# Two message-passing layers on a graph: edge pairs staged over three steps instead of five, self connection of layer 1 at later lags

## The reference

```python
def layer0(x, a, src, dst, edge_attr, edge_scalars, W):
    h = linear(x, lin1) * a                      # per node
    w = silu(edge_scalars @ fc_w1) @ fc_w2       # 224 weights per edge
    e0, e1 = edge_attr[:, :1], edge_attr[:, 1:4]
    # per edge, from h[src], w, e0 and e1: 96 scalars and 128 vectors
    mid = products(h[src], w, e0, e1)            # a cross product among them
    agg = segment_sum(mid, dst, n) / 4
    pre = self_connection(x) + linear(agg, lin2) * a
    return silu / sigmoid gates applied to pre
# layer 1: the same shape without the cross product, a mean over the edges of a node
# and a factor alpha per node in place of the gates
x = layernorm(x + layer0(...))
x = layernorm(x + layer1(x, ...))
```

## Time and profile before

| | us |
|---|---|
| median of 3 runs | 2077.51 |
| lowest and highest | 2066.84, 2082.15 |
| the profiled execution | 2061.54 (span of its trace 2059.5) |
| edges, layer 0 | 0 to about 757 |
| nodes, layer 0 | about 757 to 1097 |
| edges, layer 1 | about 1097 to 1786 |
| nodes, layer 1 | about 1786 to 2059 |

### The profile page before, as it was taken

How to read it: one execution, slowest core, us unless ns; L and a number is a source line. 1 busy time by engine, 2 the same in 40 slices (tenths; PEclk the granted TensorE clock), 3 DMA queues, 4 the chain that set the end, 5 groups by cost and what they waited for, 6 DMA issues and landing times.

```text
span 2059.5 us, 47563 instructions
## 1 busy us (share of the span) xinstructions
PE 1431.6 (70%) x10424; PEld 1270.4 (62%) x10424; DVE 1443.3 (70%) x5661; ACT 1067.1 (52%) x3600; POOL 1498.0 (73%) x2021
## 2 busy tenths in 40 slices
PE   5077887878888848778775999999999999200000
PEld 4067777767777737666654988888888888200000
DVE  5066776767777619999993766666666666199997
ACT  3033444434444317999983555555555555147676
POOL 3077877778788648888884577777777777468876
PEclk9589999999999979999997999999999999655555
DMA  9966666666666759999964677777777777499997
GB/s 388 430 150 138 135 131 136 137 137 135 131 137 138 169 128 320 322 320 319 317 237 133 165 166 174 172 170 173 175 167 171 171 172 159 80 364 406 400 390 280
DMA packets 253878, 439.88 MB, mean 214 GB/s; under 512 B 33424, under 2 KB 131152, under 8 KB 250576
## 3 DMA queue, kind: packets, MB, share of 16 engines
q1 hardware_dynamic: 150288, 306.88, 44.3%
q0 software_dynamic: 75264, 67.79, 23.8%
q10 hardware_dynamic: 28224, 64.24, 8.1%
HBM read 235.50 MB, written 203.27 MB: 213 GB/s over the span
## 4 chain that ended last, share of the span: by engine, by line
POOL 38%; issue 21%; PE 14%; ACT 9%; DMA 8%; SPq 4%; DVE 3%; ACTq 2%; POOLq 1%; another core or an unknown queue 0%; DVEq 0%
POOL table L482 16%; POOL xg L465 8%; ACT y L827 6%; DMA table<-sums,row_all 5%; POOL half_rstd L516 5%; SPq L370 3%; PE ps L642 2%; POOL gate L547 2%; PE ps L623 2%; POOL gate L538 2%; DMA dst_row<-in_dst_row 2%; ACTq L838 2%; PE ps L609 1%; PE ps L628 1%; PE ps L625 1%
## 5 line engine op out<-in xcount | busy, mean ns | idle before, releaser
L482 POOL DMA_INDIRECT table<-sums,row_all x392 | 627.9, 1602 | 306.9 <-issue 131.2
L764 ACT COPY msg<-ps 128x192 f32<-128x192 f32 (+1 forms) x196 | 57.4, 293 | 691.9 <-PE ps L642 555.9
L827 ACT ACTIVATE y<-res,norm 128x160 f32<-128x160 f32 x756 | 331.9, 508 | 133.3 <-ACT y L827 62.1
L975 DVE SCALAR_TENSOR_TENSOR x1g<-ps,a_all,x1g 128x160 f32<-128x160 f32 x392 | 132.3, 379 | 200.2 <-PE ps L662 130.3
L465 POOL DMA_INDIRECT xg<-in_x_rows,src_all x196 | 201.0, 1025 | 59.6 <-issue 57.2
L465 POOL DMA_INDIRECT xg<-x_rows,src_all x196 | 195.3, 997 | 65.0 <-issue 59.4
L623 PE MATMUL ps<-weights,midT 128*128 128x128 f32 (+1 forms) x784 | 161.7, 290 | 95.6 <-DVE msg L935 93.9
L1055 DVE BATCH_NORM_STATS2 stats<-res 128x6 f32<-128x160 f32 x784 | 195.6, 310 | 2.6
L930 DVE TENSOR_TENSOR pe<-ps,ea_all 128x192 f32<-128x192 f32 x196 | 69.4, 354 | 170.4 <-ACT msg L764 73.6
L623 PEld LDWEIGHTS ps<-weights,midT 128*128 128x128 f32 x784 | 124.5, 200 | 103.1 <-issue 95.6
L516 POOL TENSOR_TENSOR half_rstd<-var,minus_half 128x8 f32<-128x8 f32 x98 | 165.5, 1688 | 14.2
(11 more groups left out here) (115 smaller groups left out, 4465.1 us busy)
## 6 DMA issues: line engine op xcount, KB each, us to landing
...
```

The source lines that it names most:

```text
L482: pool.indirect_dma_start(out=table[l], out_offset=bass.IndirectOffsetOnAxis(ap=row_all[:, at:at + 1], axis=0), in_=sums[j % 4][:, t, 0:W] ...
L827: last = nc.scalar.activation(y[u][:, t, :], res[u][:, t, :], ACT.Identity, scale=rstd[u][:, t:t + 1], bias=shift[u][:, t:t + 1])
L975: last = stt(x1g[v][:, 2 * b + t, :], n1_ps[:, t, :], a, x1g[v][:, 2 * b + t, :], ALU.mult, ALU.add)
```

## The change

The lists of `run_stages` in the edge stages get other lags and another order. A pair's `turn_mid` and `copy_midT` go from lag 2 to lag 1, at the end of the lists; `second_map` and `copy_message` from lag 3 to 2, at their head; `message_vectors` and `message_sum` from 4 to 2, behind `compare`; `sum_pair` and `copy_sums` from 5 to 3. In layer 1 the self connection goes from lags 0, 1 and 2 to 3, 4, 5 and 6 and the store of the base from 4 to 10; x1g is used as a ring of eight buffers in place of four, with a semaphore for each.

```diff
--- before.py
+++ after.py
@@ -286,8 +286,8 @@
         s_z1 = sem("self_connection_added")
         s_x1z = sem("z_of_x1_together")
         s_n1 = sem("self_connection_done_layer1")
-        s_x1 = sem4("x1_loaded")
-        s_bstore = sem4("base_stored")
+        s_x1 = [sem(f"x1_loaded{u}") for u in range(RING)]
+        s_bstore = [sem(f"base_stored{u}") for u in range(RING)]
         s_base = [sem(f"base_loaded{u}") for u in range(RING)]
         s_nT = sem("nodes_turned")
         s_nTsb = sem("nodes_turned_copied")
@@ -377,20 +377,18 @@
                     sp.dma_start(table[1][bass.ds(m * GROUP, GROUP), :].rearrange("(p t) c -> p (t c)", t=T),
                                  zeros[:, 0:T * LAYERS[1]["ROW"]]).then_inc(s_zero[1], 16)
 
+                def store_base(g, m, u):
+                    sp.wait_ge(s_z1, 2 * (g + 1 - NG))
+                    sp.sem_inc(s_sptick, 1)
+                    sp.dma_start(base_rows[bass.ds(m * GROUP, GROUP), :].rearrange("(p t) c -> p (t c)", t=T),
+                                 x1g[u][:, :, :].rearrange("p t c -> p (t c)")).then_inc(s_bstore[u], 16)
+
                 def load_x1(g, m, u):
 
-                    v = u % 4
-                    wait_count(sp, s_bstore[v], landed(g - 4, first_of(v, 4), 4))
+                    wait_count(sp, s_bstore[u], landed(g - RING, first_of(u, RING), RING))
                     sp.sem_inc(s_sptick, 1)
-                    sp.dma_start(x1g[v][:, :, :].rearrange("p t c -> p (t c)"),
-                                 x1_rows[bass.ds(m * GROUP, GROUP), :].rearrange("(p t) c -> p (t c)", t=T)).then_inc(s_x1[v], 32)
-
-                def store_base(g, m, u):
-
-                    v = u % 4
-                    sp.wait_ge(s_z1, 2 * (g + 1 - NG))
-                    sp.dma_start(base_rows[bass.ds(m * GROUP, GROUP), :].rearrange("(p t) c -> p (t c)", t=T),
-                                 x1g[v][:, :, :].rearrange("p t c -> p (t c)")).then_inc(s_bstore[v], 16)
+                    sp.dma_start(x1g[u][:, :, :].rearrange("p t c -> p (t c)"),
+                                 x1_rows[bass.ds(m * GROUP, GROUP), :].rearrange("(p t) c -> p (t c)", t=T)).then_inc(s_x1[u], 16)
 
                 assert NP == NG
                 if l == 1:
@@ -398,7 +396,7 @@
                     for u in range(4):
                         sp.wait_ge(s_store[u], stored(NG, u))
                 run_stages(sp, base, NP, 10, [(0, load_attr), (0, load_dst_row)] +
-                           ([(0, clear_table0), (8, clear_table1)] if l == 0 else [(4, store_base), (0, load_x1)]), RING)
+                           ([(0, clear_table0), (8, clear_table1)] if l == 0 else [(10, store_base), (3, load_x1)]), RING)
 
                 W = LAYERS[l]["ROW"]
 
@@ -430,8 +428,8 @@
                     sp.dma_start(table[1][N_PAD:ROWS, :].rearrange("(p t) c -> p (t c)", p=P),
                                  zeros[:, 0:2 * LAYERS[1]["ROW"]]).then_inc(s_zero[1], 16)
                 else:
-                    for u in range(4):
-                        sp.wait_ge(s_bstore[u], landed(2 * NG - 4 + (u - 2 * NG) % 4, first_of(u, 4), 4))
+                    for u in range(RING):
+                        sp.wait_ge(s_bstore[u], landed(2 * NG - RING + (u - 2 * NG) % RING, first_of(u, RING), RING))
                     run_stages(sp, NG, NG, 10, [(0, load_base), (2, load_table)], RING)
 
             for u in range(4):
@@ -644,11 +642,11 @@
                 def turn1(g, b, u):
 
                     v = u % 4
-                    pe.wait_ge(s_x1[v], landed(g, first_of(v, 4), 4, 32))
+                    pe.wait_ge(s_x1[u], landed(g, first_of(u, RING), RING))
                     pe.wait_ge(s_x1z, g + 1 - NG)
                     wait_count(pe, s_nTsb, 2 * (g - NG) + b)
                     for t in range(2):
-                        turn(x1T_ps[:, t * P:(t + 1) * P], x1g[v][:, 2 * b + t, 0:M], ident[:, :])
+                        turn(x1T_ps[:, t * P:(t + 1) * P], x1g[u][:, 2 * b + t, 0:M], ident[:, :])
                     turn(z1T_ps, x1z[v][:, 2 * b:2 * b + 2, :], ident[:, :]).then_inc(s_nT, 1)
 
                 def nodes1(g, b, u):
@@ -680,12 +678,12 @@
                         mm(ps[:, 0:512], ident[:, :], zeros[:, 0:512], start=True, stop=True)
                     pe.wait_ge(s_res, NG)
                 if l == 0:
-                    run_stages(pe, 0, NP, 10, [(1, first_map), (0, hidden), (1, edge_weights), (0, turn_x),
-                                               (3, second_map), (2, turn_mid), (5, sum_pair)], RING)
+                    run_stages(pe, 0, NP, 10, [(2, second_map), (1, first_map), (0, hidden), (1, edge_weights), (0, turn_x),
+                                               (3, sum_pair), (1, turn_mid)], RING)
                 else:
-                    run_stages(pe, NP, NP, 10, [(1, first_map), (0, hidden), (1, edge_weights), (2, nodes1a), (0, turn_x),
-                                                (1, turn1a), (3, second_map), (2, turn_mid), (1, turn1b),
-                                                (2, nodes1b), (5, sum_pair)], RING)
+                    run_stages(pe, NP, NP, 10, [(2, second_map), (1, first_map), (0, hidden), (1, edge_weights), (6, nodes1a),
+                                                (0, turn_x), (5, turn1a), (3, sum_pair), (5, turn1b), (1, turn_mid),
+                                                (6, nodes1b)], RING)
 
                 def nodes0(g, m, u):
 
@@ -781,9 +779,9 @@
                 def copy_z1(g, m, u):
 
                     v = u % 4
-                    act.wait_ge(s_x1[v], landed(g, first_of(v, 4), 4, 32))
+                    act.wait_ge(s_x1[u], landed(g, first_of(u, RING), RING))
                     wait_count(act, s_nT, 2 * (g - 1 - NG))
-                    copy(x1z[v][:, :, :], x1g[v][:, :, M:D]).then_inc(s_x1z, 1)
+                    copy(x1z[v][:, :, :], x1g[u][:, :, M:D]).then_inc(s_x1z, 1)
 
                 def copy_nT(g, b, u):
 
@@ -800,12 +798,12 @@
                     copy_nT(g, 1, u)
 
                 if l == 0:
-                    run_stages(act, 0, NP, 10, [(0, copy_z), (1, copy_h), (0, hidden_act), (0, copy_xT),
-                                                (3, copy_message), (2, copy_midT), (5, copy_sums)], RING)
+                    run_stages(act, 0, NP, 10, [(0, copy_z), (2, copy_message), (1, copy_h), (0, hidden_act), (0, copy_xT),
+                                                (3, copy_sums), (1, copy_midT)], RING)
                 else:
-                    run_stages(act, NP, NP, 10, [(0, copy_z), (1, copy_h), (0, hidden_act), (0, copy_xT),
-                                                 (1, copy_nTa), (3, copy_message), (2, copy_midT), (0, copy_z1),
-                                                 (1, copy_nTb), (5, copy_sums)], RING)
+                    run_stages(act, NP, NP, 10, [(0, copy_z), (2, copy_message), (1, copy_h), (0, hidden_act), (0, copy_xT),
+                                                 (5, copy_nTa), (3, copy_sums), (4, copy_z1), (5, copy_nTb),
+                                                 (1, copy_midT)], RING)
 
                 def gates(g, m, u):
 
@@ -972,7 +970,7 @@
                     dve.wait_ge(s_n1, 2 * (g - NG) + b + 1)
                     for t in range(2):
                         a = a_all[:, bass.ds(m, 1), 2 * b + t:2 * b + t + 1].rearrange("p g t -> p (g t)")
-                        last = stt(x1g[v][:, 2 * b + t, :], n1_ps[:, t, :], a, x1g[v][:, 2 * b + t, :], ALU.mult, ALU.add)
+                        last = stt(x1g[u][:, 2 * b + t, :], n1_ps[:, t, :], a, x1g[u][:, 2 * b + t, :], ALU.mult, ALU.add)
                     last.then_inc(s_z1, 1)
 
                 def add_self_a(g, m, u):
@@ -983,11 +981,11 @@
 
                 if l == 0:
                     run_stages(dve, 0, NP, 10, [
-                        (4, message_vectors), (0, scale_attr), (2, compare), (4, message_sum), (2, mark_later),
+                        (0, scale_attr), (2, compare), (2, message_vectors), (2, mark_later), (2, message_sum),
                         (1, products), (2, step_rows), (3, choose_rows)], RING)
                 else:
                     run_stages(dve, NP, NP, 10, [
-                        (4, message_vectors), (2, compare), (4, message_sum), (2, add_self_a), (1, products), (2, add_self_b)], RING)
+                        (2, compare), (2, message_vectors), (2, message_sum), (6, add_self_a), (1, products), (6, add_self_b)], RING)
 
                 if l == 0:
                     dve.wait_ge(s_hid, NP)
```

## The result

| | before | after |
|---|---|---|
| median, us | 2079.83 (6 runs, 2066.84 to 2120.98) | 2316.76 (6 runs, 2312.92 to 2322.41) |
| the profiled execution | 2061.54 (span 2059.5) | 2312.97 (span 2311.0) |
| edges, layer 0 | 0 to 757.4 | 0 to 946.7 |
| nodes, layer 0 | 757.4 to 1096.9, 339.5 | 946.7 to 1286.7, 340.0 |
| edges, layer 1 | 1096.9 to 1785.9, 689.0 | 1286.7 to 2042.5, 755.8 |

The kernel is slower: 1.1145 times before, 95% interval 1.112 to 1.117. Some executions of before fall into a slower state (here 2112.78 and 2120.98 us), and every ratio in this text, like what is said of before beside an experiment, leaves such executions out. In the profiled executions that is +251.5 us of span: +189 in the edges of layer 0, +67 in those of layer 1, -5 in the rest. The prediction had +141, +119 and 0: 2337 us forecast, 2316.76 measured, with errors that partly cancel.

A forecast was written before the change was run, and what follows sets the result against it. POOL bounds the kernel before; after, one-step cycles of 8.35 and 8.0 us do. Layer 0 +141 and layer 1 +119 make +260 us: 2061.54 becomes 2322, and 16 to the median gives 2337 us, range 2235 to 2470.

The forecast's parts named there:

- POOL sets the pace before: Edge stages before: POOL needs 6.4 us a pair for two gathers and two scatters; other engines are no slower.
- a cycle of one step: Edge stages after: products through turn_mid and second_map to the next products, 8.35 us in layer 0, 7.82 in layer 1.
- The waits named beforehand: Profile after: POOL's scatter, PE's second_map and turn_mid, and DVE's add_self would wait for other engines; indirect DMAs 8 us apart.
- The branches of layer 0: Layer 0, second_map to products: through first_map, hidden and copy_h 1.9 us, through the message 1.8; nothing added.
- The side branch: Layer 0: second_map through first_map, hidden and copy_h to products, 1.9 us.
- The size of the cycle: Record lengths plus 0.15 us a handover: 8.35 us a step in layer 0, 7.82 in layer 1 before late signals.
- the rival that the prediction gave 0.07: Layer 0: PE's clock falls because of its pauses, 10.7 us a step, 218 us more, 2555 us; chance 0.07.
- 1.2 GHz throughout: Layer 0, the clock rival's case: turn_mid and second_map cost 2.37 us more a step, 218 us in all.
- 898 forecast: End of layer 0's edge stage, in us: 113 + 92 x 8.35 + 17.
- Late signals of layer 1: PE's completion signals reach DVE late, bounds 0 and about 1.4 us a step; 0.2 added, giving 8.0 us.
- The self connection at no cost: Layer 1: its later loads and stores on SP cost 0 while a 320 KB load lands within a step.
- the five short steps at its end: End of layer 1's edge stage: five added steps holding only self connection, beside the last scatters, 5 us.

The follow-up runs named there:

- the run with fillers: Kernel after with three more matmuls, results unused, ahead of turn_mid in each layer-0 step on PE: 2242.43 us.
- the five-step order: Two kernels with layer 1's pair order of before but the late self connection and ring of eight: layer-1 stage 713.5 and 717.9 us, against 696.9 before.

## Why the prediction was right, and where it was off

**POOL sets the pace before, and the new lists shut a cycle of one step.** Right, and shown: in layer 0 only opening both branches brings POOL's pace back, at the same depth. The waits named beforehand stand in the profile: the scatter for DVE's rows, second_map for copy_midT, turn_mid for the products, add_self for nodes1 (94.3 us of DVE's waiting, 1300 to 1800 us).

**The branches of layer 0.** The prediction called them a tie, 1.9 against 1.8 us, and added nothing. The side branch is the longer by 0.22 us; two runs show it (the message moved away: no gain; 0.22 us added to it: no loss in a step at full clock).

**The size of the cycle.** 8.35 us forecast, 8.02 at full clock. What was mis-sized is the way of adding: length of each record plus 0.15 us at each change of engine. By starts, turn_mid and its handover are 0.91 (0.97 in the sum), copy_midT 0.91 (1.01), second_map 1.41 (1.55), copy_h to products 0.75 (0.85), products to turn_mid 2.92 (3.00); only first_map to copy_h is longer, 1.12 (1.04). By the prediction's own terms the side branch, which closes the cycle, comes to 8.42. In layer 1 the same: 7.82 in the sum, 7.36 by starts, with first_map to edge_weights 1.57 for 1.70, nodes1a 0.93 for 1.00, add_self 0.60 for 0.69, products 1.96 for 2.07; only second_map is longer, 0.97 for 0.87. A record's length reaches into the next instruction (the end of a matmul is modelled), and a chain of them adds that up five to eight times. 92 x 0.33 = 30 us too much in layer 0, 92 x 0.46 = 42 in layer 1.

**The clock of layer 0.** The largest single miss, and the rival that the prediction gave 0.07, at a third of its price. It reasoned that pauses of 1.2 and 1.7 us are short; the trace of after has them at 0.94 and 1.67, and yet 42 of 87 steps ran partly at half clock. 67 us by the run with fillers, where "1.2 GHz throughout" would have cost 218. With it: 898 forecast, - 30 for the links, + 67 for the clock, + 12 left over for filling and draining, gives the 946.7 measured. The Trainium skill ("TensorE: Matmul & The Clock Gate", A second HAM failure mode: psum-queue depth-cycling) tells of a kernel in which short, frequent idle moments of PE make the clock go to and fro. The trace agrees: in after's layer 0 full and half clock alternate, and no pause of PE is longer than 1.74 us in the rows above. The prediction cited the section beside it and added that no row showed the like for pauses so short; the rows of after now do.

**Late signals of layer 1.** 0.2 us a step were added for them. In after they are gone: 0.16 us where before had 1.58, and the mean step, 7.41, is only 0.05 over the cycle. With the links this is all of layer 1's miss: 92 x (8.0 - 7.41) = 54 against 52 us. The prediction's reason, that the lateness shows after long unbroken runs of matmuls, is not what the traces show: 385 of before's 424 late signals of layer 1 fall between POOL's second gather and the end of its first scatter (see the last section).

**The self connection at no cost.** Right in the kernel after, and even the five short steps at its end can't be seen (751.4 against 756.7). In the five-step order it may cost something; the profiled executions say 17 to 25 us, the timed runs -6 to +14, and the record doesn't settle it.

**The range** of 2235 to 2470 held. The two errors have opposite signs, so the total flatters the sum, and that is luck: by stage it was 48 us too low and 52 too high. Another 12 of the 20 us between 2337 and 2316.76 are the step from the profiled execution to the median, put at 16 us and measured at 4.
